# A fused macaron block on one core: the last norm of two chunks is put inside the end of attention, the sigmoid product of the FFN moves to ScalarE, and four gate turns run one unit later

## Chip, cores, metric

The kernel runs on one core of a Trainium2 chip. The metric is the device time of that core in microseconds. The engines are TensorE (PE), VectorE (DVE), ScalarE (ACT), GpSimd (POOL) and SyncE (SP, which only issues DMAs here). Each runs its own instructions in order; they meet through semaphores.

## What is computed

x is 2048 tokens of 128 channels. Six blocks follow each other, every one behind a layer norm:

```python
x = x + 0.5 * moe(_layernorm(x), ...)          # 8 experts, top 2, hidden 512
x = x + rwkv(_layernorm(x), ...)               # a scan over time
x = x + 0.5 * moe(_layernorm(x), ...)
x = x + 0.5 * _L1_ffn_ref(_layernorm(x), ...)
x = x + _L1_attn_ref(_layernorm(x), ...)       # 16 heads of 64, full softmax
x = x + 0.5 * _L1_ffn_ref(_layernorm(x), ...)
# _L1_ffn_ref: integer weights times 1/127, hidden 384
gate = x @ wg.T;  up = x @ wu.T
h = silu(gate) * up
return h @ wd.T
```

## The kernel before

**Layout.** Channels lie on the 128 partitions, tokens in the free dimension, in NC = 4 chunks of 512. A matrix product of full precision is made of fp32r products: each operand is split into a high part (a copy by ACT) and a low part (a subtraction by POOL or DVE), and TensorE adds two or three products of them in one PSUM bank. There are eight banks.

**Stages.** `mixtures()` runs both mixtures and the RWKV block in 256 units ("ticks"); then come `first_ffn()`, `norm_and_project()`, `attention()` and `last_ffn()`. Each engine's block has functions of these names with its own part of the work. The order of the work on each engine is written out by hand.

**Mixtures.** In unit t, TensorE makes one first product (3 matmuls), one second product of unit t-4 (3 matmuls), and then the side steps of `route(t)` and `rwkv(t)` that are due. Constants give their places: a router pass begins at a unit of `ROUTE_AT`, and its gates, which DVE makes at `R_GATES` = 18, are turned by TensorE at `R_TURN[j]` (L829); ACT copies them out one unit later. All side steps of TensorE share bank 7. `free_side_bank(t)` lets TensorE wait, ahead of such a step, until all readers of earlier contents are done, among them the square root (`ln_std`, ACT L1251, of a norm's variance that TensorE wrote there). The RWKV output product is at `K_PROJECT_OUT`, its addition on DVE at `K_ADD`, counted from a unit of `RWKV_AT`.

**FFN of a chunk.** `gate_and_up` (L903, L904): 12 matmuls in three tiles `ht`, each into two banks. `sigmoids` (ACT, L1318). `products` (DVE): L1723 multiplies the gate with its sigmoid, L1727 that with `up`. `high_products` (ACT, L1326) and `low_product` (POOL, L657) split the result; `down` (L918, L919) is 6 matmuls, `add_down` (DVE, L1732) adds them to x. The tiles have one buffer each, so the chunks follow each other through `f_prod`, `f_lo` and `f_down`.

**A norm of a chunk.** `mean` (PE, L760), `centre` (DVE, L1549), `square` (ACT, L1219), `variances` (PE, L767, eight instructions with one column each), `deviation` (ACT square root, L1224), `factor_of` (DVE, L1558), `spread` (PE, L774, eight instructions), `normalise` (DVE, L1568 or L1565), `high_part` (ACT, L1231) and `low_norm` (POOL, L641). Norm 5 is the last, norm 3 that of the first FFN, norm 4 that of attention.

**Attention.** A head's chunk c of queries runs in 8 groups g. TensorE makes `scores_t` (L1045, L1046) and, three groups behind (`PV_LAG`), `values` (L1060, L1063); ACT makes two exponentials of 128x1024 (L1453 and L1456), POOL the low part of the second (`low_part`, L695, `p_l`), DVE the row sums (L1814, L1826). `p_h` and `p_l` have four slots. The chunk's sums leave through a DMA round trip as columns (`invert`), come back as a broadcast, POOL multiplies with them (`scale`, L718), TensorE projects (`project_out`, L1079) and DVE adds (`add_out`, L1850). For the very last chunk there is no round trip: `end_sums` spreads the sums over 128 partitions (L1156), `end_invert` divides 128x512 (L1855), `end_scale` multiplies (L1862), and `end_out` projects (L1161).

**The end.** After head 15's last group TensorE still has `values` of groups 5 to 7, the last sums and two output products. Only then does `last_ffn` begin: four means, the variances in two banks, the spreads in two other banks, then FFN chunks 0 to 3.

Of the kernel before, what the change touches and what calls it, by code (L numbers as in the profile page):

```python
# [15 lines left out]
CH = 512  # L16
# [54 lines left out]
LATE_OUT, END_SUMS, END_OUT = 6, 4, 5  # L71
VAR_BANK, SPREAD_BANK, DOWN_BANK = (4, 5, 4, 5), (6, 7, 6, 7), ((7, 7, 7, 7), (6, 7, 7, 7))
# [16 lines left out]
R_TURN = (22, 25, 22, 22, 22, 22, 21, 21)  # L89
# [4 lines left out]
K_LN, K_INV, K_EA, K_NUM, K_GATE, K_NR, K_NR2, K_OUT, K_PROJECT_OUT, K_ADD = 29, 30, 31, 32, 33, 34, 35, 39, 46, 47  # L94
# [4 lines left out]
def macaron_kernel(nc, a, out, g_scratch, l_scratch, r_scratch):  # L99
    ctx = ExitStack()  # L100
    with ctx:
# [3 lines left out]
        def sem(name):  # L105
# [102 lines left out]
        late_cen, late_sqr = low_half[:, 0:T], low_half[:, T:2 * T]  # L208
        f_sig = high_half[:, 0:HT1 * CH].rearrange("p (a n) -> p a n", a=HT1)
# [33 lines left out]
        f_ps, f_sigmoid, f_silu, f_prod, f_hi, f_lo, f_down = (  # L243
            sem("f_ps"), sem("f_sigmoid"), sem("f_silu"), sem("f_prod"), sem("f_hi"), sem("f_lo"), sem("f_down"))
# [18 lines left out]
        end_l, end_r, end_o = sem("end_l"), sem("end_r"), sem("end_o")  # L263
# [61 lines left out]
        def maxima_plan(head, c, g, has_next):  # L325

            rest = sum(map(sum, REST_OF_MAXIMA[:c])) + sum(REST_OF_MAXIMA[c][:g])
            ahead = sum(map(sum, NEXT_MAXIMA[:c])) + sum(NEXT_MAXIMA[c][:g])
            if REST_OF_MAXIMA[c][g] > 0:
                return [(head, AHEAD + rest + i) for i in range(REST_OF_MAXIMA[c][g])]  # L330
            return [(head + 1, ahead + i) for i in range(NEXT_MAXIMA[c][g])] if has_next else []

# [229 lines left out]
        def _(pool):  # L562
# [75 lines left out]
            def low_norm(j, c):  # L638

                pool.wait_ge(xh_done, NC * j + c + 1)  # L640
                nc.gpsimd.tensor_tensor(x_l[:, chunk(c)], xn[:, chunk(c)], x_h[:, chunk(c)].bitcast(fp32), ALU.subtract).then_inc(xl_done, 1)  # L641
# [95 lines left out]
            def attention():  # L737
# [8 lines left out]
                scale(HEADS - 1, NC - 2)  # L746
# [7 lines left out]
        def _(pe):  # L754
# [7 lines left out]
            def variances(k, c, bank):  # L762

                pe.wait_ge(ln_sq, NC * k + c + 1)
                for t in range(TPC):
                    tile = slice(c * CH + t * 128, c * CH + t * 128 + 128)
                    last = mm(ps[:, bank, t:t + 1], late_sqr[:, tile], inv_c[:, 0:1], start=True, stop=True)  # L767
# [123 lines left out]
            def gate_and_up(k, c, tiles=range(HT1)):  # L891

                pe.wait_ge(xl_done, NC * (2 * k + 2) + c + 1)
                for ht in tiles:
                    pe.wait_ge(f_prod, PRIME + max((k * NC + c - 1) * HT1 + ht + 1, 0))
                    if c == 0 and ht == HT1 - 1:
                        if k == 0:
                            pe.wait_ge(y_gate, 2 * E * NC)
                        else:
                            pe.wait_ge(ln_std, NC * (2 * k + 3) + NC)  # L900
# [44 lines left out]
            def last_ffn():  # L945

                for c in range(NC):
                    mean(5, c, c)
                variances(5, 0, VAR_BANK[0])
                variances(5, 1, VAR_BANK[1])  # L950
                spread(5, 0, SPREAD_BANK[0])
                pe.wait_ge(ln_std, NC * 5 + 1)
                variances(5, 2, VAR_BANK[2])
                pe.wait_ge(ln_std, NC * 5 + 2)
                variances(5, 3, VAR_BANK[3])
                spread(5, 1, SPREAD_BANK[1])
                gate_and_up(1, 0)
                pe.wait_ge(ln_out, NC * 5 + 1)
                spread(5, 2, SPREAD_BANK[2])
                gate_and_up(1, 1)  # L960
                pe.wait_ge(ln_out, NC * 5 + 2)
                spread(5, 3, SPREAD_BANK[3])
# [133 lines left out]
            def main_chunk(pair, par, c, has_next, project, late_project):  # L1096
# [3 lines left out]
                for g in range(GROUPS):  # L1100
# [28 lines left out]
                    for i, (at, kind, n) in enumerate(plan):  # L1129
# [23 lines left out]
            def end_sums(head, c, bank):  # L1153

                pe.wait_ge(all_sum, PIECES * (chunk_of(head, c) + 1))
# [808 lines left out]
```

## Time and profile before

| | us |
|---|---|
| runs (median of 3) | 2034.76 (2033.72 to 2035.59) |
| the profiled execution's own time | 2033.69 |
| its span | 2031.9 |
| mixtures | 0 to about 457 |
| first FFN and norm 4 | about 457 to 514 |
| attention, its opening included | about 514 to 1985 |
| last norm and last FFN | about 1987 to 2031.9 |

A page of the profile gives busy times and the chain of work that ended last. In a timeline a row is: start, duration, engine, line, operation, output<-input, shapes, count, and in brackets the idle time of the engine ahead of it and who ended it ("issue": nothing that the profile shows).

### The profile page before, as it was taken

The numbers are of one execution on the slowest core, as the hardware profiler recorded it, in microseconds if no ns is written. First come the engines' busy times: TensorE is split into PE (matmuls) and PEld (weight loads), VectorE is DVE, ScalarE is ACT, GpSimd is POOL, SyncE is SP. The second block draws the span as 40 slices with busy tenths as digits, with TensorE's granted clock in tenths as the row PEclk, the third lists the DMA queues.
The fourth block names the chain that finished last, engine by engine and source line by source line (L and its number), as shares of the span: only waits on it lengthen the run. The fifth ranks groups of instructions, "written<-read, shape, count | busy, mean of one in ns | idle before, by whom it ended". The sixth has DMA issues, their size and how long they took to land.

```text
span 2031.9 us, 25651 instructions
## 1 busy us (share of the span) xinstructions
PE 1968.0 (97%) x8290; PEld 1407.6 (69%) x8290; DVE 1732.9 (85%) x1964; ACT 1463.6 (72%) x1806; POOL 1564.7 (77%) x783
## 2 busy tenths in 40 slices
PE   7999999997899999999999999999999999999987
PEld 6777777785577667777667676676777677666655
DVE  5778889666799998999999899999999999999755
ACT  5465555445388887888888788878877888888864
POOL 4332333224298999999999999999999999999994
PEclk9999999998899999999999999999999999999998
DMA  6111101220503031221303122130313223130000
GB/s 193 42 43 42 37 18 30 54 43 14 119 9 74 21 73 31 56 62 34 74 15 78 25 63 54 43 73 16 74 19 73 46 46 67 25 73 18 12 16 21
DMA packets 80679, 97.85 MB, mean 48 GB/s; under 512 B 33275, under 2 KB 36779, under 8 KB 80167
## 3 DMA queue, kind: packets, MB, share of 16 engines
q1 hardware_dynamic: 80550, 96.22, 21.4%
q8 instruction: 70, 1.15, 0.2%
q14 instruction: 59, 0.48, 0.1%
HBM read 44.25 MB, written 1.44 MB: 22 GB/s over the span
## 4 chain that ended last, share of the span: by engine, by line
PE 87%; DVE 7%; issue 2%; ACT 2%; POOL 1%; DMA 0%; SPq 0%; DVEq 0%; POOLq 0%; ACTq 0%
PE ps L1045 13%; PE ps L1023 12%; PE ps L1046 12%; PE ps L1060 11%; PE ps L1063 11%; PE ps L780 5%; PE ps L782 5%; PE ps L781 5%; PE ps L1072 3%; PE ps L1079 3%; DVE m_part L1832 1%; DVE h_l L1631 1%; POOL p_l L695 1%; PE ps L1006 1%; PE ps L1007 1%
## 5 line engine op out<-in xcount | busy, mean ns | idle before, releaser
L695 POOL TENSOR_TENSOR p_l<-p_raw,p_h 128x1024 fp32r<-128x1024 f32 x512 | 1241.8, 2468 | 86.8 <-ACT p_h L1456 83.9
L1453 ACT ACTIVATE p_raw<-ps 128x1024 f32<-128x1024 f32 x512 | 567.1, 1108 | 208.2 <-PE ps L1046 207.9
L1832 DVE TENSOR_REDUCE m_part<-ps 128x1 f32<-128x1024 f32 x512 | 621.3, 1216 | 108.0 <-PE ps L1023 108.0
L1456 ACT ACTIVATE p_h<-ps 128x1024 fp32r<-128x1024 f32 x512 | 523.6, 1023 | 0.0
L1045 PE MATMUL ps<-qa,ka 128*128 128x512 f32 x1024 | 443.6, 433 | 1.7 <-issue 1.6
L1060 PE MATMUL ps<-p_h,v_hl 128*128 128x512 f32 x1024 | 403.4, 394 | 7.4 <-POOL p_l L695 7.4
L1046 PE MATMUL ps<-qb,kb 65*128 65x512 f32 x1024 | 409.2, 400 | 0.0
L1826 DVE TENSOR_REDUCE l_sum<-p_raw 128x128 f32<-128x1280 f32 x256 | 377.2, 1476 | 13.5 <-ACT p_raw L1453 13.5
L1023 PE MATMUL ps<-ka,qa 128*128 128x512 f32 x1024 | 333.8, 408 | 7.2 <-DVE m_part L1832 6.6
L1063 PE MATMUL ps<-p_l,v_hl 128*64 128x512 f32 x1024 | 320.9, 394 | 0.0
L1814 DVE TENSOR_REDUCE p_raw<-p_raw 128x128 f32<-128x1024 f32 x256 | 308.8, 1209 | 9.5 <-ACT p_raw L1453 9.5
L605 POOL TENSOR_TENSOR x<-x,y_gated 128x512 f32<-128x512 f32 x64 | 89.2, 1395 | 256.8 <-DVE y_gated L1640 256.8
L1045 PEld LDWEIGHTS ps<-qa,ka 128*128 128x128 f32 x1024 | 194.6, 190 | 115.5 <-issue 77.3
L1301 ACT ACTIVATE h_h<-ps 128x512 fp32r<-128x512 f32 x256 | 149.3, 594 | 161.1 <-PE ps L782 159.3
L1060 PEld LDWEIGHTS ps<-p_h,v_hl 128*128 128x128 f32 x1024 | 192.9, 188 | 88.5 <-issue 8.3
L1631 DVE SCALAR_TENSOR_TENSOR h_l<-ps,h_h 128x512 fp32r<-128x512 f32 x256 | 173.7, 687 | 92.4 <-ACT h_h L1301 90.0
L1023 PEld LDWEIGHTS ps<-ka,qa 128*128 128x128 f32 x1024 | 185.4, 191 | 83.7 <-DVE m_part L1832 45.9
L1046 PEld LDWEIGHTS ps<-qb,kb 65*128 65x128 f32 x1024 | 194.8, 190 | 51.9 <-issue 14.8
L1063 PEld LDWEIGHTS ps<-p_l,v_hl 128*64 128x64 f32 x1024 | 138.1, 135 | 70.0 <-issue 0.4
L780 PE MATMUL ps<-x_h,w_l 128*128 128x512 f32 x256 | 118.3, 462 | 6.6 <-DVE h_l L1631 4.5
L782 PE MATMUL ps<-x_l,w_h 128*128 128x512 f32 x256 | 101.3, 396 | 0.0
L781 PE MATMUL ps<-x_h,w_h 128*128 128x512 f32 x256 | 101.0, 394 | 0.0
(201 smaller groups left out, 2297.0 us busy)
## 6 DMA issues: line engine op xcount, KB each, us to landing
g_bc<-g_scratch SPq DMA_DIRECT2D x64, 256.0 KB, 5.8
xn<-r_scratch SPq DMA_DIRECT2D x63, 256.0 KB, 3.9
qa<-qk_hi SPq DMA_DIRECT2D x112, 128.0 KB, 2.4
ka<-qk_hi SPq DMA_DIRECT2D x56, 128.0 KB, 2.4
kb<-qk_hi SPq DMA_DIRECT2D x56, 128.0 KB, 2.4
ka<-xn SPq DMA_DIRECT2D x28, 128.0 KB, 2.4
qb<-xn SPq DMA_DIRECT2D x28, 128.0 KB, 2.4
ka<-qk_low SPq DMA_DIRECT2D x28, 128.0 KB, 3.3
```

The source lines that it names most:

```text
L695: nc.gpsimd.tensor_tensor(p_l[:, g % 4, :, :], slots(g), p_h[:, g % 4, :, :].bitcast(fp32), ALU.subtract).then_inc(pl_done, 1)
L780: mm(o, w_lo_, x_hi_, start=start, stop=False)
L1023: last = mm(ps[:, first_bank + b, :], qa[par][:, it * 128:it * 128 + 128], ka[par][:, chunk(2 * half + b)], start=True, stop=True)
L1045: mm(st, ka[par][:, jt * 128:jt * 128 + 128], qa[par][:, ds(c * CH, CH)], start=True, stop=False)
L1046: last = mm(st, kb[par][:, jt * 128:jt * 128 + 128], qb[par][:, ds(c * CH, CH)], start=False, stop=True)
L1060: return mm(ps[:, bank, :], v_hl[:, par, 2 * g + j, :], p_h[:, g % 4, j, :], start=start, stop=stop)
L1063: return mm(ps[0:DH, bank, :], v_hl[:, par, 2 * g + j, 0:DH], p_l[:, g % 4, j, :], start=False, stop=False)
L1453: af(slots(g), s_t, ACT.Exp).then_inc(raw_done, 1)
L1456: af(p_h[:, g % 4, :, :], s_t, ACT.Exp).then_inc(ph_done, 1)
L1814: nc.vector.tensor_reduce(p_raw[:, ACC, cols, 0], p_raw[:, 0:ACC, cols, :].rearrange("p g n b -> p n g b"), AX.XY, ALU.add).then_inc(half_ ...
L1826: nc.vector.tensor_reduce(l_sum[:, cols], p_raw[:, ACC:GROUPS + 1, cols, :].rearrange("p g n b -> p n g b"), AX.XY, ALU.add).then_inc(all_ ...
L1832: nc.vector.tensor_reduce(m_part[:, it, half:half + 1], ps[:, first_bank:first_bank + 2, :].rearrange("p b n -> p (b n)"), AX.X, ALU.max). ...
```

## The change

Three things are changed.

1. Four of the eight `R_TURN` constants go from 22 to 23 units, and `K_PROJECT_OUT`, `K_ADD` from 46, 47 to 48, 49.
2. ACT computes `Silu` of the gate instead of `Sigmoid`; DVE's L1723 is gone, in both FFNs.
3. The end. Chunk 0 of norm 5 runs in groups 2 to 5 of the last attention chunk, up to its variances, with buffers of its own in `v_raw` and `qk_low2`. Chunk 1's norm and the rest of chunk 0's stand between the last `values`. The last inversion is by columns: eight instructions of one column (`end_sums`), a division of 128x4, and a spread through TensorE (`end_spread`) which DVE reads from PSUM. FFN chunk 0 starts ahead of the last two output products; means and variances of chunks 2 and 3 stand within FFN chunks 0 and 1. On POOL the last `scale` is behind `low_norm(4, 0)`. ACT computes square roots twice in the stage (chunks 0 and 1, and later 2 and 3), with `Silu` between and after.

The new queues at the end, in full:

```diff
-R_TURN = (22, 25, 22, 22, 22, 22, 21, 21)
+R_TURN = (22, 25, 23, 23, 23, 23, 21, 21)
-K_LN, ..., K_OUT, K_PROJECT_OUT, K_ADD = 29, ..., 39, 46, 47
+K_LN, ..., K_OUT, K_PROJECT_OUT, K_ADD = 29, ..., 39, 48, 49
+EARLY_MEAN, EARLY_CENTRE, EARLY_SQUARE, EARLY_VAR = 2, 3, 4, 5
+END_NORM, END_SUMS, END_OUT = (4, 5, 6, 7), 6, 7
 # GpSimd
             def last_ffn():
                 low_norm(4, 0)
+                scale(HEADS - 1, NC - 2)
                 low_norm(4, 1)
                 low_product(1, 0)
                 low_norm(4, 2)
+                low_norm(4, 3)
                 low_product(1, 1)
-                low_norm(4, 3)
                 low_product(1, 2)
                 low_product(1, 3)
 # TensorE, main_chunk
+                    if last and c == NC - 1 and g == EARLY_MEAN:
+                        pe.wait_ge(s_max, PRIME + MAXIMA * HEADS)
+                        mean(5, 0, END_NORM[0])
+                    elif last and c == NC - 1 and g == EARLY_VAR:
+                        variances(5, 0, END_NORM[0])
 # TensorE, last_ffn
+                values(head, 1, c, GROUPS - 3)
+                mean(5, 1, END_NORM[1])
+                values(head, 1, c, GROUPS - 2)
+                spread(5, 0, END_NORM[0])
+                values(head, 1, c, GROUPS - 1)
+                variances(5, 1, END_NORM[1])
+                end_sums(END_SUMS)
+                spread(5, 1, END_NORM[1])
+                gate_and_up(1, 0, (0, 1))
+                end_spread(END_SUMS)
+                pe.wait_ge(o_done, NC * HEADS)
+                project_out(head, 1, c - 1, END_OUT)
+                gate_and_up(1, 0, (2,))
+                pe.wait_ge(out_add, NC * HEADS - 1)
+                end_out(END_OUT)
+                mean(5, 2, END_NORM[2])
+                mean(5, 3, END_NORM[3])
+                gate_and_up(1, 1, (0,))
+                variances(5, 2, END_NORM[2])
+                variances(5, 3, END_NORM[3])
+                gate_and_up(1, 1, (1, 2))
+                spread(5, 2, END_NORM[2])
+                spread(5, 3, END_NORM[3])
                 down(1, 0)
                 gate_and_up(1, 2)
 # ScalarE
-            def sigmoids(k, c):
+            def silus(k, c):
                 for ht in range(HT1):
                     act.wait_ge(f_ps, (k * NC + c) * HT1 + ht + 1)
-                    af(f_sig[:, ht, :], ps[:, 2 * ht, :], ACT.Sigmoid, scale=QUANT_SCALE).then_inc(f_sigmoid, 1)
+                    af(f_sig[:, ht, :], ps[:, 2 * ht, :], ACT.Silu, scale=QUANT_SCALE).then_inc(f_silu, 1)
 # ScalarE, last_ffn
+                deviation(5, 0, END_NORM[0])
+                square(5, 1)
                 high_part(4, 0)
+                copy_out(HEADS - 1, NC - 1)
+                deviation(5, 1, END_NORM[1])
                 high_part(4, 1)
+                act.wait_ge(all_sum, PIECES * NC * HEADS)
+                act.wait_ge(pl_done, GROUPS * NC * HEADS)
+                silus(1, 0)
+                square(5, 2)
+                square(5, 3)
+                act.wait_ge(pv_done, GROUPS * NC * HEADS)
                 high_products(1, 0)
+                deviation(5, 2, END_NORM[2])
+                deviation(5, 3, END_NORM[3])
+                silus(1, 1)
                 high_part(4, 2)
+                high_part(4, 3)
                 high_products(1, 1)
+                silus(1, 2)
 # ScalarE, main_chunk
+                    if last and (c, g) == (NC - 1, EARLY_SQUARE):
+                        square(5, 0)
 # VectorE, products
-                    dve.wait_ge(f_sigmoid, n + 1)
-                    stt(f_sig[:, ht, :], ps[:, 2 * ht, :], QUANT_SCALE, f_sig[:, ht, :], ALU.mult, ALU.mult).then_inc(f_silu, 1)
 # VectorE, main_chunk
+                    if last and (c, g) == (NC - 1, EARLY_CENTRE):
+                        centre(5, 0, END_NORM[0])
 # VectorE, last_ffn
+                invert(head, c - 1)
+                whole_sum(head, c, 0)
+                whole_sum(head, c, 1)
                 factor_of(5, 0)
+                centre(5, 1, END_NORM[1])
+                whole_sum(head, c, 2)
+                normalise(5, 0, END_NORM[0])
+                whole_sum(head, c, 3)
                 factor_of(5, 1)
+                end_invert(END_SUMS)
+                normalise(5, 1, END_NORM[1])
+                end_scale(END_SUMS)
+                add_out(head, c - 1, END_OUT)
+                products(1, 0, (0, 1))
+                add_out(head, c, END_OUT)
+                centre(5, 2, END_NORM[2])
+                centre(5, 3, END_NORM[3])
+                products(1, 0, (2,))
+                products(1, 1, (0,))
                 factor_of(5, 2)
                 factor_of(5, 3)
+                products(1, 1, (1, 2))
+                normalise(5, 2, END_NORM[2])
+                normalise(5, 3, END_NORM[3])
                 add_down(1, 0)
                 products(1, 2)
+# VectorE, end_invert and end_scale
-                nc.vector.reciprocal(qk_hi, ps[:, bank, :]).then_inc(end_r, 1)
+                dve.wait_ge(r_stored, 16 * (NC * HEADS - 1))
+                nc.vector.reciprocal(r_col[:, (NC - 1) % 2, :], ps[:, bank, 0:TPC]).then_inc(end_r, 1)
-                tt(at, at, qk_hi, ALU.mult).then_inc(end_o, 1)
+                tt(at, at, ps[:, bank, :], ALU.mult).then_inc(end_o, 1)
```

## Rows read from the trace of the kernel before

**Rows 1.** Page, busy time of each engine and share of the span.

```profile
PE 1968.0 (97%) x8290; PEld 1407.6 (69%) x8290; DVE 1732.9 (85%) x1964; ACT 1463.6 (72%) x1806; POOL 1564.7 (77%) x783
```

**Rows 2.** Waits of PE from 20 to 470 us: total us, times, longest.

```profile
PE ps L780 <- DVE h_l L1631: 4.5, 6, 2.2
PE ps L829 <- issue: 4.0, 4, 1.0
```

**Rows 3.** Timeline around the turn of router pass 2.

```profile
102.11 1.28 ACT L1251 ACT_TABLE_LOAD   x1
...
103.40 0.26 ACT L1251 ACTIVATE ln_s<-ps,eps 128x4 f32<-128x4 f32 x1
...
103.77 1.03 PE L829 MATMUL ps<-ident,gates 128*8 128x128 f32 x8 [0.99 <-issue]
```

**Rows 4.** Timeline of PE at unit 202: the mean behind the fourth RWKV addition.

```profile
368.95 1.02 PE L799 MATMUL ps<-x,inv_c 128*128 128x512 f32 x2
```

**Rows 5.** Timelines of the first FFN, rows of ACT, DVE and PE.

```profile
459.18 1.57 ACT L1318 ACTIVATE p_raw<-ps 128x512 f32<-128x512 f32 x3
...
459.81 0.69 DVE L1723 SCALAR_TENSOR_TENSOR p_raw<-ps,p_raw 128x512 f32<-128x512 f32 x1 [1.85 <-ACT p_raw L1318]
...
474.06 0.68 DVE L1568 TENSOR_TENSOR xn<-p_raw,ps 128x512 f32<-128x512 f32 x1
...
476.81 0.50 PE L903 MATMUL ps<-x_h,wgu 128*128 128x512 f32 x1 [2.58 <-POOL x_l L641]
```

**Rows 6.** Timeline of the end of attention.

```profile
1967.09 9.61 POOL L695 TENSOR_TENSOR p_l<-p_raw,p_h 128x1024 fp32r<-128x1024 f32 x4
...
1970.38 1.01 ACT L1456 ACTIVATE p_h<-ps 128x1024 fp32r<-128x1024 f32 x1
...
1972.09 0.47 PE L1060 MATMUL ps<-p_h,v_hl 128*128 128x512 f32 x1 [1.23 <-POOL p_l L695]
```

**Rows 7.** Chain of work that ended last, 1955 us to the end: start, us, what.

```profile
1963.81 0.24 PE ps L1046
...
1978.46 0.43 PE ps L1060
...
1980.63 3.37 DVE qk_hi L1855
...
1986.84 4.08 PE ps L760 x8
...
1992.32 1.28 ACT L1224
...
1995.62 3.20 PE ps L767 x16
1998.82 1.93 PE ps L774 x8
...
2001.50 0.63 ACT x_h L1231
```

**Rows 8.** Timeline of the last norm and the last FFN.

```profile
1990.75 1.84 PE L767 MATMUL ps<-inv_c,p_raw 128*128 128x1 f32 x16
...
2003.81 1.05 PE L774 MATMUL ps<-ident,ln_r 128*128 128x128 f32 x8
...
2011.50 0.48 PE L903 MATMUL ps<-x_h,wgu 128*128 128x512 f32 x1
...
2012.47 3.80 POOL L657 TENSOR_TENSOR p_l<-p_raw,p_h 128x512 fp32r<-128x512 f32 x3 [1.04 <-ACT p_h L1326]
...
2028.68 0.69 DVE L1732 SCALAR_TENSOR_TENSOR x<-ps,x 128x512 f32<-128x512 f32 x1 [3.02 <-PE ps L919]
```

**Rows 9.** Stretches: us, busy us of each engine, granted clock of TensorE, DMA.

```profile
1975.00:1980.00 5.00, 4.67 (x10) 2.50 (x9) 1.18 (x1) 0.60 (x1) 2.92 (x2) 0.50 0.00 0
...
1995.00:1998.00 3.00, 3.00 (x16) 3.00 (x16) 0.87 (x2) 0.89 (x2) 0.92 (x1) 0.50 0.03 5
...
2010.00:2020.00 10.00, 9.04 (x36) 5.61 (x35) 9.21 (x15) 6.22 (x12) 8.52 (x8) 1.00 0.07 27
```

More of the change, by code:

```diff
@@ L331, in maxima_plan, with centred, squared, normed @@
             return [(head + 1, ahead + i) for i in range(NEXT_MAXIMA[c][g])] if has_next else []
+        def centred(k, c):
+            return end_cen[c] if k == 5 and c < 2 else late_cen[:, chunk(c)]
+        def squared(k, c):
+            return end_sqr[c] if k == 5 and c < 2 else late_sqr[:, chunk(c)]
+        def normed(k, c):
+            return end_xn[c] if k == 5 and c < 2 else xn[:, chunk(c)]
         def wait_x(eng, k, c):
@@ L895, in gate_and_up @@
                     pe.wait_ge(f_prod, PRIME + max((k * NC + c - 1) * HT1 + ht + 1, 0))
+                    if k == 1 and c == 0:
+                        pe.wait_ge(ph_done, GROUPS * NC * HEADS)
                     if c == 0 and ht == HT1 - 1:
@@ L945, in last_ffn @@
             def last_ffn():
[L947 to L962, printed above, removed]
+                head, c = HEADS - 1, NC - 1
+                values(head, 1, c, GROUPS - 3)
[21 more added lines that the diff above has]
+                spread(5, 3, END_NORM[3])
                 down(1, 0)
@@ L1151, in main_chunk, with end_sums, end_spread @@
                             project_qk(par, n, spare)
-            def end_sums(head, c, bank):
-                pe.wait_ge(all_sum, PIECES * (chunk_of(head, c) + 1))
-                mm(ps[:, bank, :], inv_c[:, :], l_sum[:, :], start=True, stop=True).then_inc(end_l, 1)
+                    if last and c == NC - 1 and g == EARLY_MEAN:
[3 more added lines that the diff above has]
+                        variances(5, 0, END_NORM[0])
+            def end_sums(bank):
+                pe.wait_ge(out_add, NC * (HEADS - 1) + 2)
+                pe.wait_ge(all_sum, PIECES * NC * HEADS)
+                for t in range(TPC):
+                    last = mm(ps[:, bank, t:t + 1], l_sum[:, t * 128:t * 128 + 128], inv_c[:, 0:1], start=True, stop=True)
+                last.then_inc(end_l, 1)
+            def end_spread(bank):
+                pe.wait_ge(end_r, 1)
+                for t in range(TPC):
+                    last = mm(ps[:, bank, t * 128:t * 128 + 128], r_col[:, (NC - 1) % 2, t:t + 1].to_broadcast([128, 128]), ident[:, :],
+                              start=True, stop=True)
+                last.then_inc(end_bc, 1)
             def end_out(bank):
@@ L1218, in square @@
                 act.wait_ge(ln_cen, NC * k + c + 1)
-                af(late_sqr[:, chunk(c)], late_cen[:, chunk(c)], ACT.Square).then_inc(ln_sq, 1)
+                af(squared(k, c), centred(k, c), ACT.Square).then_inc(ln_sq, 1)
             def deviation(k, c, bank):
@@ L1230, in high_part @@
                 act.wait_ge(ln_out, NC * (0, 2, 3, 4, 5)[j] + c + 1)
-                af(x_h[:, chunk(c)], xn[:, chunk(c)], ACT.Copy).then_inc(xh_done, 1)
+                af(x_h[:, chunk(c)], normed((0, 2, 3, 4, 5)[j], c), ACT.Copy).then_inc(xh_done, 1)
             def high_weights(t):
@@ L1911, in attention @@
                 window(PAIRS - 1, 1, False, False, False)
-                invert(HEADS - 1, NC - 2)
-                for i in range(PIECES):
-                    whole_sum(HEADS - 1, NC - 1, i)
-                end_invert(END_SUMS)
-                end_scale()
-                add_out(HEADS - 1, NC - 2, LATE_OUT)
-                add_out(HEADS - 1, NC - 1, END_OUT)
             mixtures()
```

67 lines of the change are left out of this document (22 added, 45 removed).

## Prediction

> **What bounds the kernel now.** I read the page first, then the waits of TensorE, then the timelines of the three places that the change touches, then the chain at the end. TensorE is busy 97% of the span [rows 1], so time is gained only where it waits, where it runs at the lower clock, or where the work at the end lies in single file. The waits in the mixtures show two things that last: low parts of DVE (4.5 us in six waits) and the turn of the gates (4.0 us in four waits of at most 1.0) [rows 2]. The timeline of one of the four shows what ends it: ACT loads a table at 102.11 and writes the square root at 103.40 to 103.66, and TensorE goes on with L829 at 103.77 after 0.99 idle [rows 3]. It is `free_side_bank`: the turn of pass j falls in the unit next to the square root of an RWKV norm (25 + 22 = 47, 40 + `N_STD` = 46). The last chunk of attention is paced by POOL, whose low parts follow without a gap (9.61 us for four) while TensorE waits up to 1.23 us for each and ACT has been done with the last exponentials since 1971.4; POOL ends at 1976.7 [rows 6]. Behind that the chain is one file: last sums, a division of 3.37, an output product, four means in 4.08, a table load, variances, spreads, until chunk 2's products start at 2011.50 and the last addition ends at 2029.37 [rows 7, 8].
>
> **Part 1, the turns.** What goes: 4 waits x 0.99 = 3.96 us. One unit later TensorE arrives at the turn after six more matmuls at 0.235 apart [rows 7], 1.4 us, and the root is done 0.9 us after it arrived before, so nothing of the wait is left. What is late next: `h_l` of DVE, with four buffers, hence about three units of slack; the six waits for it [rows 2] stand elsewhere. The later `K_ADD` could hold the mean at unit 202, which starts at 368.95 [rows 4]; I work out DVE's addition to end at about 369.1, so 0 to 0.3 us lost. ACT's copy, the store of the gates and their eight loads start 1.4 us later; the first user is nine units (15 us) behind. Part 1: **-3.9**, bounds -4.0 and -2.5.
>
> **Part 2, Silu.** It removes 24 instructions of DVE of 0.69 each, 12 per FFN, and adds none: ACT makes 12 as before, three in 1.57 [rows 5]. No row shows a Silu. The bounds: as the Sigmoid (0.52 apart), or twice it (+0.52 each); I take the first, since a copy of the same shape takes 0.63 [rows 7] and an exponential of twice the columns 1.01 [rows 6]: the function makes no difference there. In the first FFN the freed DVE time is worth less than 12 x 0.6, for POOL's low parts (3.80 for three [rows 8]) become the pace: products of chunk c wait for `f_lo` of chunk c-1. I count at the longest wait: chunk 3's gate starts at 476.81 after 2.58 us idle [rows 5] because L1568 comes at 474.06, behind DVE's pairs of chunks 0 to 2. With single products, walking the four queues with the durations of the rows, L1568 starts at 472.15 and chunk 3's gate at about 474.9: 1.9 to 2.3 us earlier. After it the norm of attention is one file and carries that on. With another lie of the lower clock the same walk gives 1.0 to 2.7. Part 2 in the first FFN: **-2.0**, bounds -2.7 and +0.5 (Silu at twice the time). Of the second FFN it is counted below.
>
> **Part 3, inside attention.** Added to the last chunk: mean 0.86 and variances 0.92 on TensorE, square 0.63 on ACT, centre 0.69 on DVE. The cover is POOL's backlog: ACT has the last exponentials ready at 1971.39, POOL takes that group at 1974.3 (1967.09 and three low parts of 2.40) [rows 6], 2.9 us later. The additions on TensorE and ACT make 2.4 us if nothing overlaps, and TensorE idles 0.3 us a group besides, so POOL ends at 1976.7 as before. Cost nothing; if the cover were gone, at most 2.4 us. The additions wait for `add_out` of head 15's chunk 0, done at that chunk's start.
>
> **Part 3, the file behind it.** Walk of TensorE's queue, at the rows' rates: a matmul 0.235 at 2.4 GHz (granted 1.00) and 0.43 at 1.2 (granted 0.50) [rows 7, 9]; a mean or an output product 0.86; variances 0.92 (1.84 for 16) or 1.6; a spread 1.05 or 1.93 [rows 7, 8]. I keep the lower clock where it is now, until about 1981.2.
> - 1976.2 spread 0 (standing ahead of `values` 7), 1977.9 `values` 7, 1979.6 variances 1, 1981.3 last sums, 1982.2 spread 1, 1983.2 two tiles of chunk 0's gates, 1985.1 spread of the inverse, 1986.1 output product 2, 1986.95 third tile, 1987.9 last output product, 1988.75 means 2 and 3, 1990.6 chunk 1's first tile, 1991.5 variances 2 and 3, 1993.35 two more tiles, free at 1995.2. The division of 3.37 is gone, for 128x4 and the spread.
> - ACT from variances 3: load 1.28, two roots of 0.26 [rows 3, 7], load 1.28, Silu 0.59; DVE's product 0.69 stands ahead of the factors 2 and 3: 1998.2. So TensorE idles 3.0 us here: the wait that takes the place of those removed.
> - Spreads 2 and 3, normalise 0.68 behind two products of DVE, copy 0.63 [rows 7], POOL 1.28: chunk 2's gate at 2002.3, against 2011.50 now [rows 8], 9.2 earlier.
> - Chunks 2 and 3 take 17.87 us now (2011.50 to 2029.37) [rows 8]. DVE's pairs go, POOL's 6 x 1.27 and the ring of tiles stay: 17.1, so 0.8 more.
>
> That is -10.0. The same walk with the lower clock also from 1984.6 to 1988.0 and from 1998.2 to 2001.6 gives -7.7; with no lower clock from 1974 on, -12.5; with the lower clock twice as often, -3.2. I take the middle of the first two: **-8.8**. The walk with the old queues comes out at 2029.3 for a row that ends at 2029.37.
>
> The table loads are the point where a rule speaks against the change. A load is 1.28 us in the rows, and the next instruction of ACT starts 0.01 after it [rows 3, 7]; the last FFN has two loads now and four after, and the two more, 2.6 us, are in the walk. The Trainium skill (ScalarE: Activation LUTs, "What ACT_TABLE_LOAD costs" and "Table sets: the hidden batching unit") asks to batch by set and gives about 2.66 us per switch with a drain; by that figure, as an estimate from the page, the last FFN would gain 2.8 us less. The trace shows no such drain, so the sum goes by the row.
>
> **Sum.** -3.9 - 2.0 - 8.8 = -14.7 from the profiled execution's 2033.69 us (span 2031.9 and 1.8 around it) is 2019.0. The median of the runs is 1.07 above that execution, hence **2020.1 us**.
>
> **Rivals.**
> - *TensorE at the lower clock through much of the end.* For it: two stretches of the end run at 0.50 now [rows 9], and the new queue has many one-column instructions, which fill time without speed (the 16 of 1995.62 ran at 0.50 [rows 7, 9]). Against: from 2010 to 2020, with gaps in every tile, it ran at 1.00 [rows 9]. Tail -3.2 to -6 instead of -8.8: 2020.1 + 4.2 = 2024.3.
> - *Full clock throughout the end.* Tail -12.5 and first FFN -2.7: 2015.7. For it: fewer idle microseconds for TensorE; against: the 3.0 us wait before spread 2 stays.
> - *Silu is dearer or brings loads with it.* Twice the time, or a set without Square (one load more out and one in, in each FFN): 2.6 to 6 us, 2024. Nothing in the profile speaks for it, but no row excludes it.
> - *Slower: Silu's set holds no Copy.* Then ACT would load out and in at every chunk: 2 x 1.28 x 8 chunks = 20.5 us on ACT, which lies in the path Silu, product, copy, low part of each chunk. 2020.1 + 20.5 = 2040.6. It decides from six such pairs on (14.7 / 2.57 = 5.7, if all are exposed). Against: the copies after the Sigmoid and after the root need no load in the timeline now.
> - *The file does not get shorter:* the four means were one block and are now in the queue behind chunk 0; if the 3.0 us wait and the order of POOL (`low_norm` 0 ahead of the last `scale`) cost all that overlap brings, only parts 1 and 2 remain: -5.9, 2028.9. The walk speaks against it, since `scale` ends at 1982.1, four microseconds ahead of its user.
>
> **How the numbers follow.** Forecast 0.60, lower clock 0.17, full clock 0.10, dearer Silu 0.05, file not shorter 0.05, slower 0.03. The range takes in the full clock (2015.5) and the lower clock with part 1's and part 2's poor bounds (2026). A measurement of this kernel can tell 0.2%, 4.1 us, from no change. Faster by more than that (below 2030.7): 0.96; within: 0.01; slower: 0.03.
>
> **What would show it.** In the mixtures the four waits of L829 gone and the others unchanged, the first FFN starting 3.9 us earlier. No L1723; three Silu in about 1.57. Chunk 3's gate (L903 of the first FFN) idle 2.5 us still, but 6 us earlier in all. POOL's last `p_l` end as far behind the start of the last chunk as now. Four table loads behind the last exponential, a wait of TensorE of about 3 us ahead of spread 2, and 17 us from chunk 2's first gate to the last addition. Wrong if: more loads, a Silu above 0.7 us, granted clock 0.50 beyond the spreads, or POOL's low parts with gaps in the last chunk.

## The result, and the profile after

The changed kernel takes 2014.7 us (median of four runs, 2010.5 to 2017.8) against 2034.24 before (median of four): ratio 0.9903, 95% interval 0.989 to 0.9917, or 19.5 us less. Two repeats gave 2014.2 and 2014.04 (0.9905 and 0.9901). The prediction was 2020.1 with a range of 2015.5 to 2026.0: right in sign, 5 us short, and the median lies under the range. The profiled execution took 2017.8 us with a span of 2014.4. What lies around the span was 1.8 us in every run of the kernel before, 1.8 to 2.1 in most runs of kernels with the new end and up to 3.4 in some; I found no reason for it.

The page's line of busy times, which answers to [rows 1]:

```profile
PE 1960.9 (97%) x8304; PEld 1405.8 (70%) x8304; DVE 1712.6 (85%) x1940; ACT 1466.2 (73%) x1808; POOL 1564.9 (78%) x783
```

TensorE has 14 matmuls more and is busy 7 us less; the mean granted clock is 0.989 against 0.987. VectorE has the 24 instructions less.

The waits of TensorE from 20 to 470 us (engine, line, whom it waited for, total us, times, longest), beside [rows 2]:

```profile
PE ps L796 <- DVE h_l L1673: 4.9, 6, 2.2
...
PE ps L863 <- DVE w_base L1700: 1.1, 2, 0.6
```

The four waits at the turn are gone. Two shorter ones have come that the kernel before had not, as TensorE's timeline shows (start, us, engine, line, operation, idle before it and what ended it):

```profile
164.40 0.50 PE L796 MATMUL ps<-x_h,w_l 128*128 128x512 f32 x1 [0.46 <-DVE h_l L1673]
...
305.30 1.12 PE L863 MATMUL ps<-w_base,rwkv_w 128*128 128x512 f32 x2 [0.62 <-DVE w_base L1700]
```

The first FFN, beside [rows 5]: three Silu in the time of three Sigmoids, and chunk 3's gate 5.5 us earlier (476.81 to 471.29), behind 2.09 us of idle time.

```profile
455.62 1.57 ACT L1354 ACTIVATE p_raw<-ps 128x512 f32<-128x512 f32 x3
...
471.29 0.50 PE L921 MATMUL ps<-x_h,wgu 128*128 128x512 f32 x1 [2.09 <-POOL x_l L657]
```

The end, beside [rows 6 and 8], from the timeline of each engine:

```profile
1959.78 9.58 POOL L712 TENSOR_TENSOR p_l<-p_raw,p_h 128x1024 fp32r<-128x1024 f32 x4
...
1983.85 1.28 ACT L1260 ACT_TABLE_LOAD   x1
1985.15 0.42 ACT L1260 ACTIVATE ln_s<-ps,eps 128x4 f32<-128x4 f32 x2
1985.59 1.28 ACT L1354 ACT_TABLE_LOAD   x1
...
1987.51 0.69 DVE L1767 SCALAR_TENSOR_TENSOR p_raw<-ps,p_raw 128x512 f32<-128x512 f32 x1 [5.29 <-ACT p_raw L1354]
...
1988.34 3.78 PE L790 MATMUL ps<-ident,ln_r 128*128 128x128 f32 x16 [2.89 <-DVE ln_r L1600]
...
1994.44 0.40 PE L921 MATMUL ps<-x_h,wgu 128*128 128x512 f32 x1
...
2011.22 0.69 DVE L1772 SCALAR_TENSOR_TENSOR x<-ps,x 128x512 f32<-128x512 f32 x1 [5.12 <-PE ps L937]
```

POOL's last four low parts follow without a gap: the additions inside attention hide. Its last one ends at 1969.36, and from there the file runs to chunk 2's gate at 1994.44 and the last addition. To compare kernels I measure between such marks. The first mark is TensorE's first product of the mixtures, some 20 us into the span; a gate is the first `gate_and_up` matmul of a chunk of the first FFN; the last column is called the tail below (us):

| profiled run | first product to first gate | gate 0 to gate 3 | gate 3 to first projection | first projection to attention's first low part | attention's low parts | tail: last low part to end |
|---|---|---|---|---|---|---|
| before | 437.14 | 19.80 | 23.14 | 53.51 | 1423.24 | 55.19 |
| turns alone | 434.02 | 19.79 | 23.09 | 53.47 | 1423.54 | 55.2 |
| Silu alone | 436.01 | 17.83 | 20.71 | 51.75 | 1423.11 | 54.5 |
| new end alone | 437.31 | 19.79 | 24.67 | 53.48 | 1423.57 | 46.56 |
| changed | 433.79 | 17.84 | 21.36 | 53.48 | 1423.22 | 45.06 |
| changed, repeat | 433.91 | 17.83 | 19.93 | 52.86 | 1423.18 | 45.06 |
| changed, third | 433.81 | 17.82 | 20.70 | 54.81 | 1423.28 | 43.10 |

The columns "gate 0 to gate 3" and "attention's low parts" do what was forecast. "Gate 3 to first projection" does not: nothing in it was changed but one product less per tile, and it lost 1.8 to 3.2 us. The stage behind it, with no change at all, moved by -0.7 to +1.3 us. (Silu alone has 1.1 us less in the first column without any change there: from 60 to 70 us its granted clock is 1.00, in before 0.83.)

### The profile page after: what moved, and what is told of

It is laid out like the page before. It is cut to its first block, busy times and chain, and to the rows that moved or that the text cites. A ratio compares the mean times of both kernels' runs of the same rounds, so it can differ in the third digit from the quotient of the medians.

```text
span 2014.4 us, 25661 instructions
## 1 busy us (share of the span) xinstructions
PE 1960.9 (97%) x8304; PEld 1405.8 (70%) x8304; DVE 1712.6 (85%) x1940; ACT 1466.2 (73%) x1808; POOL 1564.9 (78%) x783
## 4 chain that ended last, share of the span: by engine, by line
PE 87%; DVE 6%; ACT 2%; issue 2%; POOL 1%; DMA 0%; POOLq 0%; SPq 0%; DVEq 0%; ACTq 0%
PE ps L1071 13%; PE ps L1049 12%; PE ps L1072 12%; PE ps L1086 12%; PE ps L1089 12%; PE ps L796 5%; PE ps L798 5%; PE ps L797 5%; PE ps L1098 3%; PE ps L1105 3%; DVE h_l L1673 1%; DVE m_part L1885 1%; PE ps L1032 1%; PE ps L1033 1%; PE ps L1031 1%
```

## The parts, each alone

The kernel before with `R_TURN` of passes 2 to 5 at 23, `K_PROJECT_OUT` 48 and `K_ADD` 49 only:

> The kernel before with part 1 alone (four gate turns one unit later, the RWKV output product and its addition two units later). Theory of the sum (each part is worth its own waits): the four waits of 0.99 us of TensorE ahead of L829 go, nothing comes back, the median is 3.6 to 3.9 us below before. Rival (the gain of a part depends on where the lower-clock stretches fall afterwards): the stages behind start 3.6 us earlier, but the end, with the old queues, is 1 to 2 us longer or shorter than before.

Measured: 2030.49 us (11 runs) against 2034.03 (15), ratio 0.9982 (0.9973 to 0.9991): -3.5. The waits of 0.99 are gone; those of 0.46 and 0.62 shown above are in this kernel too and give some back.

Silu and no L1723, in both FFNs, else as before:

> The kernel before with part 2 alone (Silu on ScalarE, VectorE's first product gone, in both FFNs, old queues otherwise). Theory of the prediction: 2.0 us less in the first FFN and about 0.8 to 1.5 in the last, -3 in all. Rival, after the stage times of the changed kernel (first FFN and norm 4 were 3.7 us shorter than before): Silu alone is worth 3.7 us there, hence -4.5 to -5.5 in all; then my walk of that stage was too short. If it is again 2.0, the other 1.7 us are the lie of the lower clock.

Measured: 2027.75 us (5 runs), 0.9969 (0.9956 to 0.9981): **-6.3**, where 2.0 were forecast for the first FFN and 0.8 for the last. The interval, 3.9 to 8.9 us, leaves out the 2.8 of the prediction and the 3 of the expectation; the rival's 4.5 to 5.5 lies in it.

The new end with Sigmoid and both products, turns as before:

> The changed kernel with parts 1 and 2 undone (old turn units, Sigmoid on ScalarE and two products on VectorE in both FFNs), so part 3 alone. By the sum -8.8 less what single products bring to the end (about 1), so -7.5 to -9 against before, with 17.9 us from chunk 2's first gate to the last addition. Rival (clock): the scatter of 7 us between runs of the changed kernel is the lower clock falling or not falling into the new end; then this kernel scatters by several us too, while the two kernels with the old end scatter by 2 us like before, and its fastest runs are 12 us below before.

Measured: 2024.99 us (5 runs, 2023.89 to 2028.03), 0.9959 (0.9946 to 0.9971): -9.0. Its runs lie 4.1 us apart, about as far as those of Silu alone (3.9), which has the old end, so the rival is not borne out here. From chunk 2's first gate to the last addition are 17.63 us, forecast 17.9.

The changed kernel again:

> The changed kernel as it is, timed again beside the three parts. If the parts add up, its distance to before is the sum of the three distances. By the clock theory another profile of the same program has its lower-clock stretches of the last 45 us elsewhere or has none, and the distance from POOL's last low part of attention to the end differs by as much: 42.6 us with the granted clock at 0.50 for 6.8 us behind the first table reload (the profile I have), about 39 to 40 us without.

Measured: 2014.2 us (4 runs), 0.9905. The three parts sum to -18.8, the whole is -19.8: within the scatter they add up. Against the forecast Silu brings 3.5 more (6.3 for 2.8), the end 1.0 more (9.0 for 8.8 less Silu's 0.8), the whole 1.0 more than the parts, and the turns 0.4 less: together the 5.1 that the forecast lacks, Silu's being the largest. The expectation counts the end to the last addition: 42.55 us in the first profile. The repeat has the same low stretch and the same tail; the one without it came with the third profile, 40.57 us.

## Where Silu's other four microseconds are

Up to chunk 3's gate Silu gains 1.97 us (19.80 to 17.83), and in the tail, with the old queues, 0.7 in its one profile. Behind the gate, VectorE's timeline of the kernel before shows the factor of norm 4 (five instructions of 128x4) beside GpSimd's low products:

```profile
484.22 0.16 DVE L1541 TENSOR_TENSOR ln_n<-ln_n,ln_r 128x4 f32<-128x4 f32 x1
484.35 3.71 POOL L657 TENSOR_TENSOR p_l<-p_raw,p_h 128x512 fp32r<-128x512 f32 x3 [3.43 <-ACT p_h L1326]
484.42 1.23 DVE L1542 TENSOR_SCALAR ln_n<-ln_n 128x4 f32<-128x4 f32 x1
485.68 0.18 DVE L1543 RECIPROCAL ln_n<-ln_n 128x4 f32<-128x4 f32 x1
485.89 0.97 DVE L1544 TENSOR_TENSOR ln_r<-ln_r,ln_n 128x4 f32<-128x4 f32 x1
...
486.91 0.58 PE L774 MATMUL ps<-ident,ln_r 128*128 128x128 f32 x1 [2.73 <-DVE ln_r L1544]
```

An operation on four columns takes 1.23 us when it starts 0.07 us after a low product of GpSimd (three in 3.71), and the next such one 0.97: both end where a low product ends. The division between them takes its 0.18. In the kernel with Silu alone:

```profile
482.51 0.17 DVE L1542 TENSOR_SCALAR ln_n<-ln_n 128x4 f32<-128x4 f32 x1
482.60 2.49 POOL L657 TENSOR_TENSOR p_l<-p_raw,p_h 128x512 fp32r<-128x512 f32 x2 [5.03 <-ACT p_h L1326]
...
482.93 0.96 DVE L1544 TENSOR_TENSOR ln_r<-ln_r,ln_n 128x4 f32<-128x4 f32 x1
...
483.94 0.82 PE L774 MATMUL ps<-ident,ln_r 128*128 128x128 f32 x5 [1.51 <-DVE ln_r L1544]
```

VectorE is free when the root comes, so L1542 starts 0.09 us ahead of GpSimd and keeps its 0.17. One of the two holds is gone, and TensorE's wait is 1.51 instead of 2.73: 1.2 us that I had not counted. The Trainium skill (SBUF — State Buffer, "SBUF: two separate sides") says that VectorE and GpSimd share a port pair under an exclusive lock, which VectorE needs for its two-port modes or for two SBUF inputs. The trace agrees: 0.17 against 1.23 and 0.16 against 0.97 for the same instructions.

The rest is TensorE's clock. In the kernel before and with matmuls added (next experiment), the stretch from gate 3 to the first projection is (stretch, us, then busy us and instructions of PE, PEld, DVE, ACT and POOL, granted clock, DMA share, GB/s):

```profile
476.81:499.95 23.14, 18.83 (x73) 13.89 (x73) 13.29 (x25) 9.04 (x18) 10.36 (x9) 0.78 0.00 1
```

```profile
477.06:497.36 20.30, 16.90 (x85) 12.27 (x85) 13.22 (x25) 9.05 (x18) 10.38 (x9) 1.00 0.00 1
```

### Matmuls added in TensorE's waits

The added function and one of its four places (8, 8, 4 and 4 matmuls):

```diff
+def fill(bank, n):
+    for _ in range(n):
+        mm(ps[:, bank, 0:384], wgu[:, 0, 0:128], wgu[:, 1, 0:384], start=True, stop=True)
...
+pe.wait_ge(rms_std, 1)
+fill(ATT_BANK[0], 8)
 spread(4, 0, ATT_BANK[0])
```

> The kernel before, with 24 matmuls of 384 columns added on TensorE in four places of the first FFN and the norm behind it (8 ahead of chunk 3's gate, 8 ahead of norm 4's first spread, 4 and 4 ahead of a mean and of the last spread). They write banks that are overwritten next, so the output is the same; each place had an idle time of TensorE of 1.5 to 2.7 us in the trace of before, and the added work is 0.6 to 1.3 us there at the full clock, twice that at the low one. Theory: the part of the gain that the forecast lacked is the clock: with fewer idle stretches of TensorE there are fewer stretches at the lower clock between chunk 3's gate and the first projection (10.3 us of them in before, 3.4 in the kernel with Silu alone). Then this kernel shows under 7 us of low clock there, the stage gate 3 to first projection is 21.5 to 22.5 us instead of 23.14, the mean clock rises above 0.986 and the time is 1 to 2 us under before, 2032 to 2033. Rival: idle time of TensorE has nothing to do with it and Silu's gain is waits alone: the same low stretches, and a time between 2034.0 and 2035.5, since the added matmuls at the low clock outgrow the waits by up to 1 us.

Measured: 2030.82 us (11 runs) against 2033.7 (15), ratio 0.9986 (0.9978 to 0.9995): **24 matmuls more, 2.9 us less**. The granted clock of the stretch went from 0.78 to 1.00 and the stretch from 23.14 to 20.30 us, more than I expected, although the wait ahead of the spread still was 1.36 behind the added work and L1542 took 1.25. The mean clock of all runs rose from 0.9859 to 0.9882.

That profile alone would not show that there is less of the lower clock: from the first projection to attention's first low part it took 54.64 us instead of 53.51, and the granted clock of that whole execution was 0.986, where before's was 0.987. Some of what left the stretch lay elsewhere in it. The rise of the mean over the runs and their time are what speaks for less of it.

> The changed kernel with 19 such added matmuls of 384 columns in the same four places (6, 5, 4, 4), in waits of 2.1, 1.5, 1.5 and 1.5 to 1.9 us. Theory of the clock: mean clock over the runs above the 0.991 of the changed kernel and a time of 2012 to 2013. Rival: the same clock and 2014.2 to 2015.

Measured: 2013.36 us (4 runs, 2011.09 to 2015.68), 0.99 (0.9886 to 0.9913); mean clock 0.9930 against 0.9913. The stretch is 19.06 us at 1.00. On the time alone, 0.8 us against this spread shows nothing.

### GpSimd held until the factor is written

```diff
 low_qk_weights(1, 1)
+pool.wait_ge(ln_rec, NC * 4 + 1)
 low_product(0, 3)
```

> The kernel before, in which GpSimd waits with chunk 3's first low product until VectorE has written the first factor of norm 4. In before that low product (1.27 us) starts at 484.35 and VectorE's maximum of 128x4 that starts at 484.42 takes 1.23 us, against 0.17 in the kernel with Silu; TensorE's wait ahead of the first spread is 2.73 us there and 1.50 with Silu. Theory: VectorE's small operation is held by GpSimd's running one. Then it takes 0.17 us here, the factor is ready 1.0 to 1.9 us earlier and the wait ahead of the spread falls to 1.0 to 1.7 us; the low products end 0.6 us later, so that the last product of that stage ends within 0.3 us of before, and the time moves by less than 1 us from its waits alone (2033 to 2034.5). Rival: the operation is long for a reason of its own: 1.2 us again, and a time 0.5 us above before.

Measured: 2030.78 us (11 runs) against 2034.51 (15), 0.9983 (0.9974 to 0.9992): **a wait added, 3.7 us less**. VectorE's and TensorE's timelines:

```profile
482.89 0.17 DVE L1543 TENSOR_SCALAR ln_n<-ln_n 128x4 f32<-128x4 f32 x1
483.09 0.18 DVE L1544 RECIPROCAL ln_n<-ln_n 128x4 f32<-128x4 f32 x1
483.31 0.16 DVE L1545 TENSOR_TENSOR ln_r<-ln_r,ln_n 128x4 f32<-128x4 f32 x1
...
483.52 1.16 PE L775 MATMUL ps<-ident,ln_r 128*128 128x128 f32 x8 [0.86 <-DVE ln_r L1545]
```

Both holds are gone and the wait is 0.86, 1.87 less. The hold by GpSimd is shown. My sum for the time was wrong again, for the same reason: the stretch ran at a granted clock of 0.99 and took 19.59 us, 3.55 less, so 1.7 us beyond the wait. Here too some of the lower clock moved: from the first projection to the first scores the kernel took 13.59 us at 0.50 instead of 12.89 at 0.74, which gives 0.7 back.

### Silu and GpSimd held

> The kernel before with Silu and one product less in both FFNs, and with GpSimd's wait for norm 4's first factor as in the run that held GpSimd. Silu alone took 6.3 us off before; the forecast had 2.0. Holding GpSimd alone took 3.7 us off. Theory: beyond its 1.96 us of waits, Silu's gain was that VectorE's small operations no longer met a running GpSimd operation and that TensorE idled less and kept its clock; both of these the held kernel has already. Then Silu over the held kernel (2030.78) is worth 2 to 3 us: 2028 to 2028.8. Rival: the two gains have nothing to do with one another and add up: 2034.3 less 6.3 less 3.7, 2024.3.

Measured: 2027.84 us (6 runs) against 2034.78 (10), 0.9966 (0.9955 to 0.9978). Silu over the held kernel is 2.9 us (3.2 when each is taken against the before of its own call), not 6.3, and the time is that of Silu alone (2027.75). So Silu's excess and the hold's gain do not add up: they are in the main the same microseconds. The waits show it, 1.51 with Silu, 0.86 held, 0.71 with both, and the mean clock over the runs rises about as far in all three: 0.9886, 0.9878 and 0.9883, from 0.985 or 0.986 before. That this is the whole of it is argued, not shown: the profile with both has 7.0 us at the lower clock in the stretch, more than Silu alone.

The same stretch in the profiled runs, us at the lower clock worked out as length x (1 - granted clock) / 0.5, and behind it the next stage, from the first projection to the first scores of attention:

| kernel | granted clock | at 1.2 GHz | stretch | wait ahead of the first spread | next stage |
|---|---|---|---|---|---|
| new end alone | 0.71 | 14.3 | 24.68 | 2.72 | 13.57 at 0.50 |
| before | 0.78 | 10.2 | 23.14 | 2.73 | 12.89 at 0.74 |
| turns alone | 0.77 | 10.6 | 23.08 | 2.73 | 12.87 at 0.74 |
| changed | 0.84 | 6.8 | 21.36 | 1.50 | 12.90 at 0.74 |
| Silu alone | 0.92 | 3.3 | 20.71 | 1.51 | 11.81 at 0.98 |
| changed, repeats | 0.91, 0.92 | 3.6, 3.3 | 19.92, 20.70 | 1.51, 1.50 | 12.15 at 0.86, 12.66 at 0.67 |
| before with Silu, GpSimd held | 0.84 | 7.0 | 21.88 | 0.71 | 12.98 at 0.74 |
| before, matmuls added | 1.00 | 0 | 20.30 | 1.36 | 12.22 at 0.80 |
| before, GpSimd held | 0.99 | 0.4 | 19.59 | 0.86 | 13.59 at 0.50 |
| changed, matmuls added | 1.00 | 0 | 19.06 | 0.64 | 11.83 at 1.00 |

Without low clock Silu is worth 20.30 - 19.06 = 1.2 us here. The kernels with the wait of 2.7 have 10 to 14 us of low clock, all others 0 to 7, each worth some 0.3 us ((24.68 - 20.30) / 14.3). Each row is one execution. That less of it lies in this stretch behind a shorter or filled wait is shown by the two additions. That there is less of it in the whole rests on the runs' mean clock and time, for the last column shows it moving into the next stage. How the chip decides is not shown, and the row with Silu and GpSimd held shows that a wait of 0.71 does not keep all of it away.

## The end

Sigmoid and two products in the last FFN only, in two cuts from ScalarE and VectorE:

```diff
-af(f_sig[:, ht, :], ps[:, 2 * ht, :], ACT.Silu, scale=QUANT_SCALE).then_inc(f_silu, 1)
+af(f_sig[:, ht, :], ps[:, 2 * ht, :], ACT.Silu if k == 0 else ACT.Sigmoid,
+   scale=QUANT_SCALE).then_inc(f_silu if k == 0 else f_sigmoid, 1)
...
+if k == 1:
+    dve.wait_ge(f_sigmoid, n + 1 - HT1 * NC)
+    stt(f_sig[:, ht, :], ps[:, 2 * ht, :], QUANT_SCALE, f_sig[:, ht, :], ALU.mult, ALU.mult).then_inc(f_silu, 1)
```

> The changed kernel with Sigmoid and the two VectorE operations in the last FFN only; Silu stays in the first. If Silu is worth in the last FFN what the tails say (46.6 us from the last low part to the end in the kernel with the new end alone, 45.06 with Silu), the time is 1.5 us over the changed kernel, 2015.7. Rival: the tail there is paced by GpSimd and Silu is worth nothing, 2014.2. What is left of Silu's gain, 4 to 5 us, then lies in the first FFN and the norm behind it.

Measured: 2017.38 us (4 runs, 2015.79 to 2019.5), 0.992: 3.2 above the changed kernel, where the runs of either lie some 4 apart. The tail is 46.57 us against 45.06, the 1.5 expected. But it was granted 0.91, and those two tails of the changed kernel 0.85. Its third profile, shown below, has 0.91 too and a tail of 43.10: at a like clock Silu is worth 3.5 us here, which fits the 3.2 of the runs. So in the new queues more of Silu's gain lies in the last FFN than the 0.8 of the forecast; how much, between 1.5 and 3.5, is not settled by single profiles.

The old division of 128x512 in the new queues, with one matmul that spreads the sums ahead of it in place of the eight by columns and of the spread of the inverse:

> The changed kernel with the last inversion as it was: one matmul that spreads the sum of exponentials over 128 partitions and a division of 128x512 (3.4 us on VectorE), in place of the division by columns and the spread by matmul. VectorE starts it at about the place of the division by columns (1970.64 in the second profile of the changed kernel, 3.1 us after the last low part ended), so normalise of chunk 1 moves from 1971.64 to about 1974.0, its copy and low part 2.4 us later, and the scaling of the last output to about 1974.9 instead of 1974.35. TensorE can start chunk 0's gate but waits for the output, so I expect the tail from the last low part to the end to grow by 0.3 to 1.2 us (45.06 to 45.4 to 46.3) and a time of 2014.5 to 2015.5. Rival: the division is fully hidden behind the gate, the Silu table load (1.28 us) and the products: 2014.2. Rival: all 3.4 less 1.5 us show: 2016.2.

Measured: 2015.35 us (4 runs), 0.9906 (0.9892 to 0.9919). VectorE and TensorE there:

```profile
1972.68 3.36 DVE L1906 RECIPROCAL qk_hi<-ps 128x512 f32<-128x512 f32 x1 [0.62 <-PE ps L1187]
...
1976.73 0.47 PE L921 MATMUL ps<-x_h,wgu 128*128 128x512 f32 x1 [0.48 <-DVE v_raw L1607]
...
1981.13 1.12 PE L776 MATMUL ps<-x,inv_c 128*128 128x512 f32 x2 [1.31 <-DVE x L1900]
```

Of its 3.36 us TensorE sees two waits, 1.79 in all, less the 1.05 of the spread that goes. The tail is 45.07, as in the changed kernel, but at a granted clock of 0.89 against 0.85; 1.2 us over 2014.2 is within the scatter. So the columns are worth about a microsecond, which these runs can't tell from none or two: by far the most of the 9 us is the overlap of norm and gates, not the smaller division.

Two reorderings of VectorE. The first puts the divisions of chunks 2 and 3 ahead of chunk 1's first product; the second, which the cut shows against the changed kernel, also puts the normalising of chunk 2 there and that of chunk 3 ahead of the last two products:

```diff
 products(1, 0, (2,))
-products(1, 1, (0,))
 factor_of(5, 2)
 factor_of(5, 3)
-products(1, 1, (1, 2))
 normalise(5, 2, END_NORM[2])
+products(1, 1, (0,))
 normalise(5, 3, END_NORM[3])
+products(1, 1, (1, 2))
```

> The changed kernel with the two small divisions of chunks 2 and 3 of the last norm put ahead of chunk 1's first product on VectorE. In the changed kernel's trace TensorE waits 2.89 us ahead of the spread of chunk 2 (start 1986.44) for a division that stands behind a product that waits for Silu of chunk 1, while the deviations were ready 2.5 us earlier. If that wait sets the end, the spread starts some 2.4 us earlier, the tail from the last low part to the end falls from 45.06 to 42.6 to 43.5, and the time is 2012 to 2013. Rival: ScalarE's Silus of chunk 1 stand ahead of the copies of chunks 2 and 3 anyway and GpSimd paces the rest: tail 44.5 to 45.1, time 2014.

Measured: 2013.3 us (4 runs), 0.9899 (0.9884 to 0.9915); tail 42.91, as expected.

> The changed kernel with the two divisions of chunks 2 and 3 and the normalising of chunk 2 ahead of chunk 1's first product on VectorE. In the run with the divisions alone put first, the tail from the last low part to the end fell by 2.15 us (45.06 to 42.91), but TensorE then waited 2.31 us for chunk 2's normalised values, which stood behind three products that wait for Silu. Expected: normalising starts 2.3 us earlier, its copy on ScalarE follows the Silus directly, 1.6 us earlier, tail 41.1 to 41.6, time 2010 to 2012.5. Rival: GpSimd's chain of low products then paces all of it, tail 42.5 to 43: 2012 to 2013.

Measured: 2013.93 us (4 runs, 2013.26 to 2014.39), 0.9898 (0.9884 to 0.9911); tail 41.15, as expected, and the wait of 2.89 is 0.25, at the higher clock:

```profile
1986.04 2.05 PE L790 MATMUL ps<-ident,ln_r 128*128 128x128 f32 x16 [0.25 <-DVE ln_r L1600]
...
1987.24 0.69 DVE L1610 TENSOR_TENSOR xn<-p_raw,ps 128x512 f32<-128x512 f32 x1 [1.10 <-PE ps L790]
```

But the time hardly moved. Two things hide it: what lies around the span was 2.4 to 3.0 us in these four runs, and the lower clock elsewhere (mean 0.9895).

> The kernel with both reorderings and 19 added matmuls in TensorE's waits of the first FFN and norm 4 (6, 5, 4, 4 as in the changed kernel with added matmuls). Adding them cost nothing where there were waits and took 2.9 us off the kernel before, 0.8 us off the changed one. Theory of the clock: 1 to 2 us under the kernel with both reorderings, mean clock 0.993 or more, 2009 to 2011. Rival: the changed kernel has so few low stretches in that stage that nothing is left to gain: the same time as without within 0.5 us.

Measured: 2011.35 us (4 runs, 2010.84 to 2011.75), 0.9885 (0.9872 to 0.9899); tail 41.15, stretch 19.06 at clock 1.00, mean clock 0.9918: 2.6 us under the kernel without the added matmuls, of which 1.8 lie in the span and the rest around it.

> The changed kernel with the two reorderings of the last norm, 16 added matmuls (6, 2, 4, 4) and GpSimd's wait for norm 4's first factor. In the changed kernel one of VectorE's five small operations there still took 0.96 us. Theory: 0.8 us off the wait ahead of the first spread, 2009.5 to 2011. Rival: the product behind it becomes late by GpSimd's later start, 2011.4 or up to 0.8 above.

Measured: 2009.86 us (4 runs, 2008.76 to 2010.79) against 2034.78, **0.9881** (0.9866 to 0.9896), mean clock 0.9943.

> The changed kernel once more, for comparison with the two others of this call on the same chip: 2013.5 to 2015 us, 0.9905 of before, mean clock 0.990 to 0.992.

Measured: 2014.04 us (4 runs, 2012.64 to 2015.75), 0.9901. So the version with both reorderings, the 16 added matmuls and the hold beats the changed kernel by 4.2 us on the same chip, and their runs do not overlap. This repeat's profile also shows what the clock alone does to the tail. Its spreads behind the same wait:

```profile
1989.09 2.05 PE L790 MATMUL ps<-ident,ln_r 128*128 128x128 f32 x16 [2.89 <-DVE ln_r L1600]
```

The 16 go through in 2.05, and the stretch from 1987.6 to 1993.0 is granted 1.00; in the first profile 1987.6 to 1994.4 is granted 0.50 and they take 3.78. Tail 43.10 against 45.06 for the same program.

## Why the prediction was short, step by step

- **Turns, -3.9 (bounds -4.0 to -2.5): -3.5 measured.** The waits went as worked out. "What is late next" was not free: waits of 0.46 and 0.62 appeared at `h_l` and `w_base`; I had seen no new one but the mean at unit 202.
- **Silu up to chunk 3's gate, -2.0 (1.9 to 2.3): 1.97.** Silu costs what Sigmoid does, three in 1.57, with no further load for Square or Copy. Both rivals on its price fall. The Trainium skill (ScalarE: Activation LUTs, "ACT is a hardware spline evaluator") says that the time of an element does not depend on the function; the trace agrees, 1.57 for three of either.
- **"After it the norm of attention is one file and carries that on": the step that failed.** The file did not just move, it got shorter: 1.2 us because one operation of VectorE no longer met GpSimd's, and 0.6 to 2 us more where TensorE ran 3 to 7 us there at 1.2 GHz instead of 10. In the profile of Silu alone the next stage shows it too, 11.81 us at a granted clock of 0.98 instead of 12.89 at 0.74. My bounds of the term (-2.7 to +0.5) covered the clock inside the FFN only and put what lies behind it at nothing. Silu alone was -6.3 where it should have been -2.8. In the changed kernel the gain from gate 3 to attention's first low part depends on the execution: 1.8, 3.9 and 1.1 us in the three profiles.
- **Inside attention, 0: right.** 1423.22 us against 1423.24, POOL without a gap.
- **The end, -8.8: measured -9.0 alone without Silu, -10.1 in the tail with it,** in two profiles, and -12.1 in the third. In size these are the walk with the clock as now (-10.0) and at full clock (-12.5). That the first fits is partly luck: the walk has the lower clock until 1981.2 and none later, and the trace has none from 1969.4 to 1987.6 and 0.50 from there to 1994.4, at the spreads. I took a middle below both, so this term too was short, by 1.3 to 3.3. The wait of 3.0 ahead of spread 2 was 2.89; chunks 2 and 3 took 17.47 us (1994.44 to 2011.91), forecast 17.1. The four table loads are there and cost 1.28 each, 0.02 ahead of the next instruction; the 2.66 per switch that the Trainium skill gives (ScalarE: Activation LUTs, "What ACT_TABLE_LOAD costs") do not show, and the end gained more than the sum by the row, not 2.8 less.
- **Rivals.** "Full clock throughout the end" (2015.7) was the nearest, for part of its reason: the end had it up to chunk 2's gate in one of three profiles, and the stretch behind the first FFN in none, though it had less of the lower clock in all. The lower clock at the spreads, which the walk of -7.7 has, came in two of three, but the end gained 10.1 even so; the slower case and "the file not shorter" did not come. Of the signs of being wrong one was there: 0.50 beyond the spreads, from 2008.0 to the end.

In numbers, by the marks: the repeat's span is 19.3 us shorter than before's, 4.6 more than forecast. Of it the stretch behind the first FFN is 3.2 (23.14 to 19.93), the stage behind that 0.7 and the end 1.3 (10.1 less 8.8), less 0.7 by which the turns came short in the profile (3.2 of 3.9). In the third profile the same terms are 2.4, -1.3, 3.3 and -0.6. So what the forecast lacks is Silu's effect outside its own FFN and the lower clock; how the 5 us divide between the file of norm 4 and the end differs from execution to execution.

## What to carry to other kernels

A stretch in single file does not only pass an earlier start on: look at each of its waits for who else runs beside the small operations, and put a term with its own bounds for the clock, since the same program's tail took 43.1 or 45.1 us. Where TensorE waits 1 to 3 us in such a file, a few useless matmuls in the wait, or a wait on GpSimd that keeps it off VectorE's small operations, can be worth as much as removed work (2.9 and 3.7 us here, the four turns 3.5); both are cheap to try. A wide operation that is replaced by a small one is worth only the wait it left behind, here about one microsecond of 3.36.

## What the runs showed of the hardware that I had not expected

- TensorE's mean granted clock differs between runs of one program (0.983 to 0.989 before, 0.988 to 0.995 changed). Over the 140 runs of the experiments, taken within each kernel, 0.001 more goes with 0.47 us less; the 0.0055 between before (0.9855) and changed (0.991) would be 2.6 us by that, an estimate.
- Adding 24 matmuls made the kernel 2.9 us faster (interval 1.0 to 4.5), adding one wait 3.7 us (1.6 to 5.3).
- A low stretch that leaves one stage can turn up in the next: with GpSimd held the stretch went from 0.78 to 0.99 and the stage behind it from 0.74 to 0.50.
- A maximum of 128x4 on VectorE takes 0.17 us alone and 1.23 beside a running GpSimd subtraction; a division of the same size keeps its 0.18, and the two products of an FFN tile (128x512, one input from PSUM) kept 0.66 to 0.69 throughout.
